# Second output buffer and a delayed subtraction in the weight quantiser of a transformer layer on eight cores

## The reference, cut to what matters

```python
def absmean_quant(w):                       # both FFN weights
    scale = jnp.mean(jnp.abs(w))
    mask = (jnp.abs(w) >= scale * 0.7).astype(w.dtype)
    return jnp.sign(w) * mask

# per batch element: x [2048, 2048], w1 [8192, 2048], w2 [2048, 8192]
q, k, v = x @ Wq, x @ Wk, x @ Wv
scores  = (q.T @ k) / 8.0                   # over the sequence: [2048, 2048]
attn    = softmax(scores, -1) @ v.T         # transposed back afterwards
x2  = layernorm(x + attn.T @ Wo)
h   = gelu(x2 @ absmean_quant(w1).T + b1)
out = layernorm(x2 + h @ absmean_quant(w2).T + b2)
```

## Time and profile before

| what | us |
|---|---|
| measured times, two runs | 3739.62 and 4132.4, median 3936.01 |
| the profiled execution's own time | 3738.87 |
| its span, core 0 | 3737.3 |
| spans of the eight cores | 3701.4 to 3737.3 |
| TensorE busy | 3195.8 (86%) |
| VectorE busy | 1258.0 (34%) |
| ScalarE busy | 736.4 (20%) |

### The profile page before, as it was taken

How to read it: one execution, slowest core, us unless ns; L and a number is a source line. 1 busy time by engine, 2 the same in 40 slices (tenths; PEclk the granted TensorE clock), 3 DMA queues, 4 the chain that set the end, 5 groups by cost and what they waited for, 6 DMA issues and landing times. The chain is left out here.

```text
span 3737.3 us, 37492 instructions; the slowest of 8 cores (3701.4 to 3737.3 us)
## 1 busy us (share of the span) xinstructions
PE 3195.8 (86%) x14917; PEld 1446.4 (39%) x14917; DVE 1258.0 (34%) x1362; ACT 736.4 (20%) x1065; POOL 94.9 (3%) x166
## 2 busy tenths in 40 slices
PE   0997999945885897199699999999969999899997
PEld 0443444412332443044344444444434444344443
DVE  0111211102444455355443344333413333333333
ACT  1344523440111121045411111111100000300003
POOL 0000000000000000000000000000000000000000
PEclk9999999977997999599899999999989999999998
DMA  9899956974445444666465666555554322643232
GB/s 196 224 274 277 279 140 181 268 216 103 128 126 179 146 141 142 151 225 237 173 195 190 196 194 185 187 195 196 185 193 158 135 102 101 215 168 135 80 123 91
DMA packets 357615, 656.84 MB, mean 176 GB/s; under 512 B 177152, under 2 KB 234560, under 8 KB 332864
## 3 DMA queue, kind: packets, MB, share of 16 engines
q1 hardware_dynamic: 238704, 297.85, 24.5%
q0 software_dynamic: 41648, 184.60, 19.0%
q10 hardware_dynamic: 77088, 171.98, 13.8%
HBM read 536.98 MB, written 150.99 MB: 184 GB/s over the span
## 5 line engine op out<-in xcount | busy, mean ns | idle before, releaser
L943 PE MATMUL psH<-big,w1sl 128*128 128x512 bf16 x4096 | 886.5, 380 | 11.4 <-DMA w1sl<-w1q_h 11.4
L1037 PE MATMUL psF<-w2g,hg 128*128 128x512 bf16 x4096 | 889.8, 380 | 0.0
L943 PEld LDWEIGHTS psH<-big,w1sl 128*128 128x128 bf16 x4096 | 401.2, 98 | 496.3 <-issue 14.6
L1037 PEld LDWEIGHTS psF<-w2g,hg 128*128 128x128 bf16 x4096 | 400.2, 98 | 489.4 <-issue 11.5
L241 DVE TENSOR_TENSOR qout<-qmask 128x1024 bf16<-128x1024 f32 x256 | 313.8, 1226 | 677.8 <-DMA w2q_h<-qout 479.9
L1087 DVE TENSOR_TENSOR oacc<-psF,oacc 128x2048 f32<-128x2048 f32 x112 | 256.6, 2292 | 588.5 <-PE psF L1037 588.5
L437 ACT ACTIVATE qmask<-sbin 128x1024 f32<-128x1024 f32 x256 | 269.8, 1054 | 404.6 <-DMA sbin<-w1t 179.7
L304 PE MATMUL psA<-wbuf,big 128*128 128x512 bf16 x1024 | 228.0, 384 | 105.9 <-DMA wbuf<-wq 99.0
L513 PE MATMUL psS<-big,qsl 128*128 128x512 bf16 x1024 | 237.5, 397 | 47.1 <-DMA qsl<-q_h 47.1
L960 ACT ACTIVATE hstg<-psH,b1sb 128x2048 bf16<-128x2048 f32 x64 | 125.9, 1967 | 745.1 <-PE psH L943 745.1
L668 PE MATMUL psO<-big,atsl 128*128 128x512 bf16 x1024 | 226.2, 382 | 49.6 <-DMA big<-v_h 28.9
(11 more groups left out here) (115 smaller groups left out, 1361.6 us busy)
## 6 DMA issues: line engine op xcount, KB each, us to landing
w2g<-w2q_h SPq DMA_DIRECT2D x16, 4096.0 KB, 13.1
sbin<-w1t SPq DMA_DIRECT2D x64, 512.0 KB, 7.4
sbin<-w1t ACTq DMA_DIRECT2D x64, 512.0 KB, 7.2
sbin<-w2t SPq DMA_DIRECT2D x64, 512.0 KB, 5.8
sbin<-w2t ACTq DMA_DIRECT2D x64, 512.0 KB, 6.0
qin<-w1t POOLq DMA_DIRECT2D x32, 1024.0 KB, 6.6
w1q_h<-qout SPq DMA_DIRECT2D x64, 512.0 KB, 6.9
w1sl<-w1q_h SPq DMA_DIRECT2D x64, 512.0 KB, 5.4
```

What stands on the lines that cost most here:

```text
L943: mm = t.matmul(ps[:, nb * 512:nb * 512 + 512], w1sl[:, (f_m % 2) * 2048 + d_k * P: (f_m % 2) * 2048 + d_k * P + P], big0[:, d_k * S + nb ...
L1037: mm = t.matmul(ps[:, nb * 512:nb * 512 + 512], hg[:, slot * 8192 + f_k * 1024 + j * P: slot * 8192 + f_k * 1024 + j * P + P], w2g[:, slot ...
```

## The change

- `qout` grows from two tiles to four, so it holds two pairs (8 KB more, in two bf16 buffers that share the space in turn). Tile i uses quarter i mod 4, pair p half p mod 2.
- The second comparison writes bf16 straight into the quarter of `qout`. The subtraction reads `qmask` or `qmask2` (by the parity of i) and this quarter, and writes the quarter in place.
- The wait for a free `qout` moves from the subtraction to the second comparison, and it is now for spill(p-2) instead of spill(p-1).
- The subtraction of a tile is held back in a list: TT(i-1) is emitted after TS1(i) and TS2(i). Only at the end of p2, p3, p4 and f1 is the last one flushed.
- To make room, `x2b` in p4 goes from three slots to two, and the transposes run two rows behind the matmuls instead of three.

```diff
@@ emit_quant_spills, emit_quant_vec
-                    c_wq.issue(eng, wq_pair_dst(p), qout[:])
+                    c_wq.issue(eng, wq_pair_dst(p),
+                               qout[:, (p % 2) * 2048:(p % 2) * 2048 + 2048])
...
+            q_pend = []
+
+            def emit_quant_tt(v):
+                i, mka, need = q_pend.pop(0)
+                qo = qout[:, (i % 4) * 1024:(i % 4) * 1024 + 1024]
+                v.wait_ge(g_qm.h, need)
+                v.tensor_tensor(qo, mka[:], qo, op=ALU.subtract).then_inc(v_qt.h, 1)
+                v_qt.inc(1)
+
+            def emit_quant_flush(v):
+                while q_pend:
+                    emit_quant_tt(v)
...
-                    if i >= 1:
-                        v.wait_ge(v_qt.h, i)
+                    if i >= 2:
+                        v.wait_ge(v_qt.h, i - 1)
...
-                    v.tensor_scalar(qmask[:], src, tbc[:, 4 * j:4 * j + 1],
+                    mka = qmask if i % 2 == 0 else qmask2
+                    v.tensor_scalar(mka[:], src, tbc[:, 4 * j:4 * j + 1],
...
-                    v.tensor_scalar(qmask2[:], src, tbc[:, 4 * j + 2:4 * j + 3],
+                    if i >= 4:
+                        c_wq.wait_item(v, i // 2 - 2)
+                    v.tensor_scalar(qout[:, (i % 4) * 1024:(i % 4) * 1024 + 1024],
+                                    src, tbc[:, 4 * j + 2:4 * j + 3],
...
-                    v.wait_ge(g_qm.h, g_qm.v)
-                    if i >= 2:
-                        c_wq.wait_item(v, i // 2 - 1)
-                    v.tensor_tensor(
-                        qout[:, (i % 2) * 1024:(i % 2) * 1024 + 1024],
-                        qmask[:], qmask2[:], op=ALU.subtract).then_inc(v_qt.h, 1)
-                    v_qt.inc(1)
+                    q_pend.append((i, mka, g_qm.v))
+                    if len(q_pend) > 1:
+                        emit_quant_tt(v)
...
@@ after the tile loops of p2, p3, p4 and f1
+                                emit_quant_flush(v)
...
@@ p4
-                         nc.sbuf_tensor("x2b", [P, 3 * 2048], BF16) as x2b, \
+                        x2b = ec4(nc.sbuf_tensor("x2b", [P, 2 * 2048], BF16))
...
-                                if s_m >= 3:
-                                    x2_transposes(s_m - 3)
-                            x2_transposes(nS - 3)
+                                if s_m >= 2:
+                                    x2_transposes(s_m - 2)
...
-                                if s_m >= 3:
-                                    s.wait_ge(t_tr4.h, s_m - 2)
+                                if s_m >= 2:
+                                    s.wait_ge(t_tr4.h, s_m - 1)
...
-                                if s_m >= 3:
-                                    x2fm_evacs(s_m - 3)
-                            x2fm_evacs(nS - 3)
+                                if s_m >= 2:
+                                    x2fm_evacs(s_m - 2)
```

More of the change, by code:

```diff
@@ L459, in _ @@
                         a_tcp.inc(1)
-                with nc.sbuf_tensor("qout", [P, 2 * 1024], BF16) as qout, \
+                with nc.sbuf_tensor("qout", [P, 4 * 1024], BF16) as qout, \
                      nc.sbuf_tensor("qin2a", [P, 2 * 1024], F32) as qin2:
@@ L708, in _ @@
                                     a_oev.inc(1)
-            with nc.sbuf_tensor("qout2", [P, 2 * 1024], BF16) as qout, \
+            with nc.sbuf_tensor("qout2", [P, 4 * 1024], BF16) as qout, \
                  nc.sbuf_tensor("qin2b", [P, 2 * 1024], F32) as qin2:
@@ L713, in build_nc @@
                     QT4_LO = QT_P2 + QT_P3
[L714 to L723, removed]
-                         nc.sbuf_tensor("x2b", [P, 3 * 2048], BF16) as x2b, \
-                         nc.Block("p4", no_gpsimd_drain=True) as blk:
+                    with contextlib.ExitStack() as st4:
+                        ec4 = st4.enter_context
+                        psy0 = ec4(nc.psum_tensor("psy0", [P, 512], F32))
+                        psy1 = ec4(nc.psum_tensor("psy1", [P, 512], F32))
+                        psy2 = ec4(nc.psum_tensor("psy2", [P, 512], F32))
+                        psy3 = ec4(nc.psum_tensor("psy3", [P, 512], F32))
+                        psy4 = ec4(nc.psum_tensor("psy4", [P, 512], F32))
+                        psy5 = ec4(nc.psum_tensor("psy5", [P, 512], F32))
+                        psT4 = ec4(nc.psum_tensor("psT4", [P, 2048], BF16))
+                        xres = ec4(nc.sbuf_tensor("xres", [P, 2 * 2048], F32))
+                        wobuf2 = ec4(nc.sbuf_tensor("wobuf2", [P, 16384], BF16))
+                        x2t = ec4(nc.sbuf_tensor("x2t", [P, 2 * 2048], F32))
+                        x2b = ec4(nc.sbuf_tensor("x2b", [P, 2 * 2048], BF16))
+                        blk = ec4(nc.Block("p4", no_gpsimd_drain=True))
                         @blk.gpsimd
@@ L760, in x2_transposes @@
                                     t.wait_ge(a_tfx.h, pm)
-                                xb = x2b[:, (pm % 3) * 2048:(pm % 3) * 2048 + 2048]
+                                xb = x2b[:, (pm % 2) * 2048:(pm % 2) * 2048 + 2048]
                                 for d_k in range(nE):
@@ L886, in _ @@
                                 s.wait_ge(v_x2.h, s_m + 1)
-                                if s_m >= 3:
-                                    s.wait_ge(t_tr4.h, s_m - 2)
-                                s.copy(x2b[:, (s_m % 3) * 2048:(s_m % 3) * 2048 + 2048],
+                                if s_m >= 2:
+                                    s.wait_ge(t_tr4.h, s_m - 1)
+                                s.copy(x2b[:, (s_m % 2) * 2048:(s_m % 2) * 2048 + 2048],
                                        x2t[:, (s_m % 2) * 2048:(s_m % 2) * 2048 + 2048]
```

## The result

The changed kernel is **1.0197 times** as long as the kernel before, 95% interval 1.0173 to 1.0221, over 11 and 10 runs taken in turn. Its median is 3827.72 us, its profiled execution 3829.71 us. Some executions on this chip are disturbed (3896 to 4383 us for the changed kernel, and 4132 us of the two behind the median of 3936 us shown for the kernel before), and the ratio leaves them out. Against 3749 us, the mean of the other runs of before, the change costs 74 us.

The account below looks back on a forecast made before the run. It took f1 as TensorE-bound, p2 as waiting for qsl and p4's start as waiting for p3's quantiser. Terms 168 - 73 + 1.5 - 2 - 4 = +91 us on 3738.9 gave 3830 us, range 3790 to 3885.

Parts of the forecast that it names:

- The mechanism of p2: In p2, spill(e-1) waits until behind score row e and holds up the next qsl load, making 14 rows serial chains.
- The size of p2: In p2, a cycle of 29.1 us for each of 14 rows, costing +168 us, bounds +142 and +205.
- Issue of qsl to the first matmul: 6.8: In each p2 row, the time from issuing the q load to TensorE's start: 6.8 us, bounds 5.6 and 9.1.
- 64 matmuls, 16.5 with the hand-over: In each p2 row, matmuls after idle time, up to the next maximum, take 16.5 us, bounds 15.8 and 16.8.
- case B: Rival for p2: with no load ahead, spill and qsl go at full rate; p2 +119, total 3781 us; chance 0.16.
- The comparison into bf16: VectorE's second comparison, now writing bf16, takes 0.81 us; at 1.23 the p2 cycle gains 0.4, +6 in all.
- The missing wait between comparison and subtraction: On VectorE, the delayed subtraction starts 0.72 us after TS2 instead of 0.97; otherwise p2 would be 3.5 us longer.
- p3: The quantiser's period in p3 falls to 6 to 7 us, so it finishes before TensorE and p4 starts earlier: -73 us.
- The start of p3: At p3's wait for v, one more 1 MB load may fall in: +1.5 us, bounds 0 and 3.3.
- p4: In p4, -2 us in the loop and -4 from one fewer transposes-and-evacuations behind the last matmul.
- f1: In f1, VectorE waits for no TensorE result, so the delayed subtraction costs nothing: 0.
- Slower by over 2%: Whole kernel: measured more than 2% slower than before, that is above 3814 us; chance 0.77.

Follow-up runs that it names:

- The gate alone: Kernel before, with only one wait added: in p2 SyncE holds spill(e-1) until both comparisons of tile 2e are done; ratio 1.0399.
- the run with the load first: Changed kernel with SyncE's two p2 transfers swapped: qsl waits for v_qt itself and goes ahead of spill(e-2); p2 402.8 us against 413.3.
- flushed rows: Changed kernel with the held-back subtraction flushed at the end of every score row of p2; 3661.35 us, ratio 0.9742 to the kernel before.

## Why the prediction was right and where it was off

**The mechanism of p2: right.** Each link is in the timeline: maximum to the end of the subtraction 5.32 us (foretold 5.32), to the issue of qsl 0.52 (0.50), 14 rows, each spill 5.4 us behind the start of the maximum. The gate alone, put into the kernel before, costs 142 us.

**The size of p2: the step that failed.** "Issue of qsl to the first matmul: 6.8" was 5.74 us in the mean of the 112 rows (5.7 to 5.9 by core). "64 matmuls, 16.5 with the hand-over" was 15.9. Together the cycle is 27.4 us (27.6 on core 6) instead of 29.1, and the term +144 instead of +168: of the 24 us the load makes 15 and the matmuls 9.

In the load it was the base that was mis-sized. With nothing ahead of it in its queue, qsl landed in 4.6 us (the run with the load first), where I had put in the 5.4 of w1sl; the spill's share was 0.9 for my 1.1, the hand-over 0.25 for 0.3. And 5.4 was no price of a lone load: it is the median of w1sl on core 0 among its neighbours in f1, which is 4.8 to 7.4 on the other cores of the same profile, with single loads down to 4.5. In the matmuls I had gone towards the row behind 29 us of idle time (16.65); behind 11.7 us they took what they took behind 4 (15.84 up to the next maximum). The load came out at the quick end, towards case B, though still within my bounds for the forecast (5.6 and 27.2). The formula of the Trainium skill (DMA: Bandwidth & Descriptors, Anatomy of one DMA) that I set beside case B is given there for transfers issued by GpSimd, while spill and qsl are SyncE's.

**The comparison into bf16**, for which no row existed, takes 0.81 us like the one into float32, and the subtraction 1.22. Both were the values taken.

**The missing wait between comparison and subtraction**: 952.49 to 953.21 is 0.72 us, where it was 0.97. The rule of the Trainium skill (VectorE: DVE Perf Modes, The DRAIN you can't avoid) that the semaphore costs nothing extra, measured there on a row of copies, does not hold for this pair; the trace of the kernel before was the better guide.

**p3: right, -73.7 for -73.** The period is 6.1 us for a forecast of 6 to 7, and the barrier is now set by TensorE's products. The run with one pair shows the depth as the cause. The hand-over took 4.2 us instead of 4.84.

**The start of p3: too small**, +4.8 for +1.5 with an upper bound of 3.3. The mechanism (weight loads share the DMA engines with v) is shown by the run that holds them: 13 us less. Its size I had capped at one more load, but one more spill comes with it. The hold takes four loads and one spill out of the stretch, 4.5 MB for 13.4 us; 1.5 MB would be 4.5 us by this, an estimate that is near the 4.8.

**p4: -4.2 for -6.** The evacuation saved behind the last matmul is there, 3.7 us, in every kernel with two slots of x2b (36.1 to 36.8 us up to f1 against 40.2). (`qout` grows by 4 KB in each partition, not 8, and the slot given up in p4 is these 4 KB.) The -2 in the loop came out as -0.5 over a stretch that also holds the first row's wait for Wo, in the changed kernel 15.9 us on core 0 and 18.7 on core 6; a term of 2 us can't be read from it. **f1: right**, no change; TensorE works 886.7 of 887 us.

**The total.** Forecast 3830 us, +91; the profiled execution took 3829.71. That they agree is luck: the sum started from a run of before 10 us below the mean of its like, the profiled execution is 7 us above the mean of its own, and 5 us are p1's. The stages sum to +70 without p1, the ratio gives +74. "Slower by over 2%" was too sure at 0.77: with 1.97% the change stands just within 2%, its interval on both sides of it. The forecast number also lies below the median of 3936 us shown for the kernel before; read against that median it would have said "faster". The sum was meant against 3739.

## What to carry to other kernels

When a result is handed on one step later, look at everything that stands behind its consumer in that queue, not at the consumer: here a spill that nobody waited for held the load that everybody waited for. Count the signals by loop iteration; a delay of 2 us that crosses a wait for the next iteration is a delay of a whole iteration. Judge a mixed edit by its parts: without the delay the edit gave 1.6% (0.9835), the delay on top of it turned that into a loss of 2% (1.0197), and one line separated them. And when you price a transfer from the length of a stage, read the pauses and the matmuls apart: a pause that shrinks can be paid for in part by a lower clock behind it.

## What the runs showed of the hardware

- Pauses of TensorE and the clock behind them, counted in p2 over all cores of three kernels (before, flushed rows, no delay). Behind pauses under 2.0 us the matmuls ran at full clock in 27 of 27 cases (14.0 us a row, 27.8 for two). Behind 2.0 to 3.4 us they did in 34 of 49, behind 3.4 to 4.0 us in 4 of 34, behind 4.0 to 6.1 us in none of 75. The others took 29.1 to 30.7 us for two rows, at a granted clock of 0.94 down to 0.91 in the rows looked at, and about 2 us more than at full clock in the mean. So pauses of the same length came out both ways, and there is no sharp edge.
- The longer of two long pauses was not the dearer one for the matmuls. Behind 11.7 us (changed kernel) 64 of them took 15.7 us at a clock of 0.89, behind 10.7 us (gate alone) 16.6 at 0.84, behind 10.4 us (load first) 16.3 at 0.86, each the mean of 112 rows.
- A load of 512 KB in rows of 256 bytes landed 4.6 us after its issue with nothing ahead of it, 5.5 with 512 KB just ahead in SyncE's own queue, and 8.6 where GpSimd had also issued 1 MB 1.3 us ahead. The same 1 MB issued 1.7 us behind it delayed it by nothing that could be measured (413.9 against 413.3 us over 14 rows).
- From the issue of a spill to its landing the median was 6.9 us in the kernel before and 3.4 us after, for the same bytes. In p3 the spill is issued 0.9 us behind a weight load in the kernel before and 3.6 us behind one in the changed kernel. Without the delay, with two pairs of `qout`, it is 0.9 us again, and the median from issue to landing is 8.0 us.
